# Softmax attention: splits and normalisations on GpSimd, product copies on ScalarE, projections cut into single contractions

## The reference, cut to what matters

```
xn  = layer_norm(x) * w + b
q,k,v = xn @ Wq + bq, xn @ Wk + bk, (xn @ Wv + bv) * mask
y   = softmax(q k^T + (1 - mask) * -big) v          per head
h   = silu(layer_norm(y) * scale(emb) + shift(emb))
out = x + h @ W_out + b_out
```

## Time and profile before

| what | us |
|---|---|
| median of 3 runs | 3429.45 (3423.07 to 3432.16) |
| span of the profiled execution | 3412.4 |
| busy in the span: PE, DVE, ACT, POOL | 2677.2, 2564.3, 2151.3, 1715.5 |
| softmax attention, first x load issued to last result | 1470.9 to 2221.0 |

### The profile page before, as it was taken

How to read it: one execution, slowest core, us unless ns; L and a number is a source line. 1 busy time by engine, 2 the same in 40 slices (tenths; PEclk the granted TensorE clock), 3 DMA queues, 4 the chain that set the end, 5 groups by cost and what they waited for, 6 DMA issues and landing times. The chain is left out here.

```text
span 3412.4 us, 37646 instructions
## 1 busy us (share of the span) xinstructions
PE 2677.2 (78%) x11156; PEld 1441.3 (42%) x11156; DVE 2564.3 (75%) x3375; ACT 2151.3 (63%) x3536; POOL 1715.5 (50%) x1221
## 2 busy tenths in 40 slices
PE   5787588888888888838888888848877788787875
PEld 4555244444444444422333333224444444444443
DVE  2444288888888898947777777538988888888895
ACT  0333478878878778613555555547876776767772
POOL 0000077867768778930000000027887877877785
PEclk9999699999999999967998989969999899989998
DMA  2000101011111111135444444010111111111111
GB/s 89 25 25 31 66 32 51 32 52 49 42 51 40 44 39 52 39 69 82 76 76 76 75 76 70 20 66 32 48 41 58 53 47 53 40 58 51 41 61 45
DMA packets 104194, 176.59 MB, mean 52 GB/s; under 512 B 10741, under 2 KB 91421, under 8 KB 95166
## 3 DMA queue, kind: packets, MB, share of 16 engines
q1 hardware_dynamic: 99775, 161.69, 17.7%
q0 software_dynamic: 4224, 12.59, 1.2%
HBM read 139.70 MB, written 34.14 MB: 51 GB/s over the span
## 5 line engine op out<-in xcount | busy, mean ns | idle before, releaser
L1037 POOL TENSOR_TENSOR l_h<-l_h,l_c_all 128x512 f32<-128x512 f32 x1024 | 1481.3, 1457 | 459.0 <-DVE l_h L966 430.8
L966 DVE TENSOR_TENSOR_SCAN l_h<-l_dA,l_ps_dbu 128x512 f32<-128x512 f32 x1024 | 1218.3, 1207 | 254.1 <-PE l_ps_dbu L1196 157.2
L838 ACT ACTIVATE l_dub<-l_duT,l_b_tok 128x512 f32<-128x512 f32 x1024 | 726.0, 713 | 336.7 <-PE l_ps_dbu L1196 330.6
L1196 PE MATMUL l_ps_dbu<-ident,l_dub 128*128 128x128 f32 x4096 | 644.7, 291 | 257.6 <-DVE l_h L966 175.6
L1196 PEld LDWEIGHTS l_ps_dbu<-ident,l_dub 128*128 128x128 f32 x4096 | 500.7, 148 | 683.6 <-DVE l_h L966 331.9
L852 ACT ACTIVATE l_dA<-l_dt,l_a_neg 128x512 f32<-128x512 f32 x1024 | 726.4, 713 | 0.2
L1628 ACT ACTIVATE l_probs<-l_ring 128x512 f32<-128x512 f32 x512 | 284.2, 598 | 301.4 <-PE l_ring L1752 298.7
L1183 PE MATMUL l_ps_y<-l_h,ident 128*128 128x512 f32 x768 | 430.2, 644 | 51.9 <-DVE l_h L931 51.4
L1461 DVE TENSOR_REDUCE l_q_max<-l_ring 128x1 f32<-128x512 f32 x512 | 327.5, 681 | 144.1 <-PE l_ring L1745 139.4
L996 POOL DMA_INDIRECT l_x_in<-x_dram,l_idx_x x32 | 37.3, 1166 | 735.9 <-DMA l_idx<-in_idx 729.6
L931 DVE TENSOR_TENSOR l_h<-l_h 128x512 f32<-128x512 f32 x384 | 350.5, 916 | 11.8 <-POOL l_h L1037 11.3
(11 more groups left out here) (237 smaller groups left out, 3000.9 us busy)
## 6 DMA issues: line engine op xcount, KB each, us to landing
...
```

The lines of the kernel that those rows point to most:

```text
L838: return act.activation(dub[:, n % 2, t, :], duT[:, p, t, :], ACT.Copy, scale=b_tok[:, p, t, n:n + 1])
L966: dve.tensor_tensor_scan(h[:, h_slot(s), :], dA[:, s % DA_RING, :], ps_dbu[:, dbu_slot(s), :], 0.0, ALU.mult, ALU.add).then_inc(scan_ok, 1)
L1037: pool.tensor_tensor(h[:, h_slot(s), :], h[:, h_slot(s), :], c_all[:, (n // C_GROUP) % 2, n % C_GROUP, :], ALU.mult).then_inc(hc_ok, 1)
L1196: last = pe.transpose(ps_dbu[:, dbu_slot(s), t * P:(t + 1) * P], dub[:, n % 2, t, j * P:(j + 1) * P], ident[:])
```

## The change

All of it lies in `softmax_attention`.

- GpSimd gets a queue of work: the second and third part of each split (`rest_parts`), the same for the maxima (`max_rest`), and both normalisations (`ln_apply`, `ln2_apply`). VectorE keeps the first subtraction of each (`split`, `max_parts`). `rest` has two buffers in place of one.
- `products_out` moves from VectorE to ScalarE.
- `project` is cut into its two contractions k = 0, 1 and `tokens` (for `v_rows` and `project_out`) into its four token blocks; each piece stands behind a step of its own.
- All four lists get new step numbers, which now count single steps s. The SP queue keeps its order. `rows` and `row_rest` become views of `probs`.

```diff
-rest = sb("rest", [P, T])
+rest = sb("rest", [P, DH, T])
...
+def ln_apply(b):
+    pool.wait_ge(rstd_ok, b + 1)
+    pool.sem_inc(passed_p, 1)
+    for t in range(TB):
+        last = pool.tensor_scalar(x_in[:, t, :], x_in[:, t, :], moments[:, t, 0:1], rstd[:, t:t + 1], ALU.subtract, ALU.mult)
+    last.then_inc(xn_ok, 1)
...
+def rest_parts(b, i, g):
+    n = b * 2 * DH + i * DH + g + 1
+    pool.wait_ge(rest_ok, n)
+    pool.sem_inc(passed_p, 1)
+    pool.tensor_copy(parts[:, i, 1, g, :], rest[:, g, :]).then_inc(p2_ok, 1)
+    pool.wait_ge(p2_ok, n)
+    pool.sem_inc(passed_p, 1)
+    pool.tensor_tensor(parts[:, i, 2, g, :], rest[:, g, :], parts[:, i, 1, g, :], ALU.subtract).then_inc(p3_ok, 1)
...
+def max_rest(b, g):
+    n = b * GROUPS + g + 1
+    pool.wait_ge(mr_ok, n)
+    pool.sem_inc(passed_p, 1)
+    pool.tensor_copy(m_parts[:, g, 1, :], m_rest[:]).then_inc(m2p_ok, 1)
+    pool.wait_ge(m2p_ok, n)
+    pool.sem_inc(passed_p, 1)
+    pool.tensor_tensor(m_parts[:, g, 2, :], m_rest[:], m_parts[:, g, 1, :], ALU.subtract).then_inc(m3_ok, 1)
...
+def run(b, p, has_post, has_next, has_after):
+    max_rest(b, 1)
+    if has_after:
+        ln_apply(b + 2)
+    max_rest(b, 2)
+    if has_post:
+        ln2_apply(b - 1)
+    if has_after:
+        rest_parts(b + 2, 0, 0)
+    max_rest(b, 3)
+    if has_after:
+        rest_parts(b + 2, 0, 1)
+    if has_next:
+        max_rest(b + 1, 0)
+    if has_after:
+        rest_parts(b + 2, 1, 0)
+        rest_parts(b + 2, 1, 1)
...
-def ln_stats(b):
-    dve.wait_ge(x_ld, b * 16 + 16)
-    for t in range(TB):
+def ln_stats(b, t2):
+    if t2 == 0:
+        dve.wait_ge(x_ld, b * 16 + 16)
+    for t in (2 * t2, 2 * t2 + 1):
         last = dve.bn_stats(stats[:, t, :], x_in[:, t, :])
-    last.then_inc(st_ok, 1)
+    if t2:
...
-    if not (first(b) and i + g == 0):
-        dve.wait_ge(p3_ok, n - 1)
-    dve.scalar_tensor_tensor(rest[:], halves[g][:], bias, parts[:, i, 0, g, :], ALU.add, ALU.subtract).then_inc(rest_ok, 1)
-    dve.wait_ge(rest_ok, n)
-    dve.tensor_copy(parts[:, i, 1, g, :], rest[:]).then_inc(p2_ok, 1)
-    dve.wait_ge(p2_ok, n)
-    dve.tensor_tensor(parts[:, i, 2, g, :], rest[:], parts[:, i, 1, g, :], ALU.subtract).then_inc(p3_ok, 1)
+    if not (first(b) and i == 0):
+        dve.wait_ge(p3_ok, n - DH)
+    dve.scalar_tensor_tensor(rest[:, g, :], halves[g][:], bias, parts[:, i, 0, g, :], ALU.add, ALU.subtract).then_inc(rest_ok, 1)
...
-def products_out(b, g):
-    n = b * GROUPS + g
-    dve.wait_ge(pv_ok, n + 1)
-    if not (first(b) and g == 0):
-        dve.wait_ge(y_tr, n)
-    dve.tensor_copy(yT[:], ps_y[:]).then_inc(yt_ok, 1)
...
-        if i in (14, 22, 30): products_out(b, i // GU - 1)
-        if i in (16, 24, 31): quotient(b, p, (i + 1) // GU - 2)
-        if i == 2: max_parts(b, 1)
-        if has_after:
-            if i == 4: ln_stats(b + 2)
-            if i == 12: ln_apply(b + 2)
-        if has_post:
-            if i == 6: products_out(b - 1, GROUPS - 1)
-            if i == 8: quotient(b - 1, 1 - p, GROUPS - 1)
-            if i == 9: ln2_stats(b - 1, 1 - p)
-            if i == 11: ln2_apply(b - 1, 1 - p)
-        if i == 10: max_parts(b, 2)
-        if has_post and i in (17, 19): result(b - 1, (i - 17) // 2)
-        if i == 18: max_parts(b, 3)
-        if has_after:
-            if i == 24: split(b + 2, 0, 0)
-            if i == 26: split(b + 2, 0, 1)
-            if i == 27: split(b + 2, 1, 0)
-            if i == 31: split(b + 2, 1, 1)
-        if i == 27 and has_next: max_parts(b + 1, 0)
+            s = 2 * i + half
+            if has_after:
+                if s in (1, 2): ln_stats(b + 2, s - 1)
+                if s == 3: ln_moments(b + 2)
+            if s == 4: max_parts(b, 1)
+            if has_post:
+                if s == 15: quotient(b - 1, 1 - p, GROUPS - 1)
+                if s in (16, 17): ln2_stats(b - 1, s - 16)
+                if s == 18: ln2_moments(b - 1)
+            if s == 19: max_parts(b, 2)
+            if has_after and s == 21: split(b + 2, 0, 0)
+            if s in (31, 47, 63): quotient(b, p, s // (2 * GU) - 1)
+            if has_post and s in (34, 36): result(b - 1, (s - 34) // 2)
+            if s == 39: max_parts(b, 3)
+            if has_next and s == 51: max_parts(b + 1, 0)
+            if has_after:
+                if s == 49: split(b + 2, 0, 1)
+                if s == 53: split(b + 2, 1, 0)
+                if s == 62: split(b + 2, 1, 1)
...
+def products_out(b, g):
+    n = b * GROUPS + g
+    act.wait_ge(pv_ok, n + 1)
+    if not (first(b) and g == 0):
+        act.wait_ge(y_tr, n)
+    act.activation(yT[:], ps_y[:], ACT.Copy).then_inc(yt_ok, 1)
...
-        if has_next and i in (7, 9): v_part(b + 1, 1 - p, (i - 7) // 2)
-        if has_post:
-            if i == 10: ln_rstd(b - 1, moments2, mom2_ok, rstd2, ln_b, rstd2_ok)
-            if i == 14:
+            s = 2 * i + half
+            if has_after and s == 5: ln_rstd(b + 2, moments, mom_ok, rstd, ln_a, rstd_ok)
+            if has_post and s == 11: products_out(b - 1, GROUPS - 1)
+            if has_next and s in (12, 15): v_part(b + 1, 1 - p, (s - 12) // 3)
+            if has_after:
+                if s in (16, 17): xnT_half(b + 2, s - 16)
+                if s == 20: first_part(b + 2, 0, 0)
+            if has_post and s == 21: ln_rstd(b - 1, moments2, mom2_ok, rstd2, ln_b, rstd2_ok)
+            if s in (27, 43, 59): products_out(b, s // (2 * GU) - 1)
+            if has_post and s == 28:
                 for h in range(DH):
                     silu_half(b - 1, h)
-        if has_after:
-            if i == 5: ln_rstd(b + 2, moments, mom_ok, rstd, ln_a, rstd_ok)
-            if i in (19, 20): xnT_half(b + 2, i - 19)
-            if i == 23: first_part(b + 2, 0, 0)
-            if i == 25: first_part(b + 2, 0, 1)
-            if i == 26: first_part(b + 2, 1, 0)
-            if i == 31: first_part(b + 2, 1, 1)
+            if has_after:
+                if s == 47: first_part(b + 2, 0, 1)
+                if s == 51: first_part(b + 2, 1, 0)
+                if s == 61: first_part(b + 2, 1, 1)
...
-def project(b, i, g):
-    if first(b) and i + g == 0:
+def project(b, i, g, k):
+    if first(b) and i + g + k == 0:
         pe.wait_ge(w_ld, 48)
-    pe.wait_ge(xnT_ok, b * DH + DH)
-    take(halves[g], rest_ok, b * 2 * DH + i * DH + g + 1)
+    pe.wait_ge(xnT_ok, b * DH + k + 1)
+    if k == 0:
+        take(halves[g], rest_ok, b * 2 * DH + i * DH + g + 1)
     weight = wq if i == 0 else wk
+    last = pe.matmul(halves[g][:], weight[:, k, g * P:(g + 1) * P], xnT[:, k, :], start=(k == 0), stop=(k == DH - 1),
+                     skip_group_check=True)
+    if k == DH - 1:
+        last.then_inc(qk_mm, 1)
...
-        if has_post and 2 <= i < 2 + TB: times_v(b - 1, 1 - p, GROUPS - 1, i - 2)
-        if i >= GU and 2 <= i % GU < 2 + TB: times_v(b, p, i // GU - 1, i % GU - 2)
-        if i == 1: max_rows(b, 1)
-        if has_post and i == 7: turn(b - 1, GROUPS - 1)
-        if has_next and i in (6, 8): v_rows(b + 1, (i - 6) // 2)
-        if i == 9: max_rows(b, 2)
-        if has_post and i in (12, 13): yn_half(b - 1, 1 - p, i - 12)
-        if i in (15, 23, 31): turn(b, i // GU - 1)
-        if has_post and i in (16, 17): project_out(b - 1, i - 16)
-        if i == 17: max_rows(b, 3)
-        if has_after:
-            if i in (18, 19): xn_half(b + 2, i - 18)
-            if i == 22: project(b + 2, 0, 0)
-            if i == 24: project(b + 2, 0, 1)
-            if i == 25: project(b + 2, 1, 0)
-            if i == 30: project(b + 2, 1, 1)
-        if has_next and i == 26: max_rows(b + 1, 0)
+            s = 2 * i + half
+            if s == 1: max_rows(b, 1)
+            if has_next and s in (0, 2, 12, 14): v_rows(b + 1, (0, 2, 12, 14).index(s))
+            if has_post and s in (4, 6, 8, 10): times_v(b - 1, 1 - p, GROUPS - 1, (s - 4) // 2)
+            if has_post and s == 13: turn(b - 1, GROUPS - 1)
+            if has_after:
+                if s in (15, 16): xn_half(b + 2, s - 15)
+                if s in (18, 19): project(b + 2, 0, 0, s - 18)
+            if s == 17: max_rows(b, 2)
+            if s >= 2 * GU and s % (2 * GU) in (4, 6, 8, 10): times_v(b, p, s // (2 * GU) - 1, (s % (2 * GU) - 4) // 2)
+            if has_post and s in (25, 27): yn_half(b - 1, 1 - p, (s - 25) // 2)
+            if s in (29, 45, 61): turn(b, s // (2 * GU) - 1)
+            if has_post and 32 <= s < 32 + TB: project_out(b - 1, s - 32)
+            if s == 37: max_rows(b, 3)
+            if has_next and s == 49: max_rows(b + 1, 0)
+            if has_after:
+                if s in (44, 46): project(b + 2, 0, 1, (s - 44) // 2)
+                if s in (48, 50): project(b + 2, 1, 0, (s - 48) // 2)
+                if s in (59, 60): project(b + 2, 1, 1, s - 59)
```

121 lines of the change are left out of this document (69 added, 52 removed).

## The result

The changed kernel took 3454.31 us (4 runs, 3447.41 to 3461.93), the kernel before 3427.01 beside it: a ratio of 1.0085, 95% interval 1.0061 to 1.011. That is **slower by 0.85%**, 21 to 38 us. The forecast was 3427.6, no change, with 3450 as its upper end.

The account below looks back on a forecast made before the run. TensorE was taken to lead, VectorE close behind, with a DMA floor before step 32. 1.8 - 7.1 + 5 x (-8.3 + 10.0) - 2.6 - 3.0 + 0.5 = -1.9 took 3429.45 to 3427.6 us; range 3402 to 3450.

Parts of the forecast that it names:

- C: Piece of a body from the first DMA of `stack` to step 32: held by transfers, so no change, 28.5 to 29.5 us.
- the DMA floor: Transfers from `stack` to the split maxima landing at step 32: a bound on C that no faster engine lowers.
- the wait for x: VectorE at the early statistics in bodies 1 to 5: idle 7.6 us until the load of x lands.
- Bodies 6 and 7 and the tail: Bodies without splits or x lose only copy and `ln2_apply` on VectorE: -3, between 0 and -6; tail +0.5.
- Start: Before body 0: normalisation on GpSimd after its fills and slower splits, less a projection and a shorter `max_parts`: +1.8 us.
- Body 0: First body, no wait for x: A -8.3, and +1.2 in B for statistics preceding `max_parts`, together -7.1 us.
- A: Piece from step 32 to the last split: transposes, a projection and pauses go, falling 8.3 to about 38 us.
- B: Piece from the last split to the first DMA of `stack`: +10.0, to 17.0 us against a mean of 7.05.
- smaller waits: Waits between pairs in A that shorter blocks avoid: 0.9 us a body, between 0 and 2.5.
- the handover of 2.1 us: Splits ending on GpSimd: its copy 0.65, subtraction 1.29 and two handovers 0.15 delay the load of x by 2.1 us.
- no relief of A: Slower rival: VectorE, still with splits at steps 49, 53, 62, holds the ring; A falls only 5; 3447 us, chance 0.10.
- The clock: Slower rival: half clock after pauses lasts 8 to 12 us a body, if A exceeds 40; 3442 us, chance 0.15.

Follow-up runs that it names:

- e8: Changed kernel with everything behind the normalisation of y three steps later, that normalisation still on GpSimd: 3429.8 us, 1.0021 of the kernel before.
- e1: Changed kernel with both normalisations (of x and of y) back on VectorE: 3419.8 us, 0.9992 of the kernel before.
- e2: Changed kernel with x loaded a body ahead, normalisations left on GpSimd: 3402.3 us, 0.9933 of the kernel before.
- e3: Changed kernel with both normalisations back on VectorE and x loaded a body ahead: 3375.7 us, 0.9851 of the kernel before.
- e5: Changed kernel with only the normalisation of y back on VectorE, that of x still on GpSimd: 3425.7 us, 1.0014 of the kernel before.
- e4: Kernel before with only the statistics of x moved from behind step 4 to behind step 0: 3459.1 us, 1.0105 of the kernel before.
- e9: e3 with its single contractions and token blocks joined again into larger blocks: 3393.9 us, 0.9918 of the kernel before.

## Why the prediction was wrong

- **C** ("the DMA floor stays: 0", the floor ending last by an estimated 2): **this step failed.** C was 32.4, 3 us more, five times 3 = 15 of the 16 by which bodies 1 to 5 were missed. The floor is there (29.4 in e8), but the step counted only what moves on TensorE and forgot the normalisation of y, which feeds its transposes at steps 25 and 27. It was moved to GpSimd and given no duration of its own anywhere in the body. The slack of 2 wasn't there either. With y back in time (e1) the Silu block, and not the floor, still ends C at 30.0; without the wait for x C falls to 30.2 (e2), without both to 28.2 (e3). So the slow clock behind the wait for x, which the floor was to swallow, reached into C.
- **Bodies 6 and 7 and the tail** (-3 and +0.5): +13.9, of which e1 takes back 14.3 and e5, with y alone, 13.7. The same omission: the work was booked as one that VectorE loses, not as one that TensorE waits for. The tail alone has a wait of 8.4 us for 4.8 before.
- **Start** (+1.8): +3.7 up to step 0 of body 0 (104.0 for 100.3). "For doing it then" had been given 1.8 us, where GpSimd needs 4.84, twice; over nine profiles the normalisation of x on GpSimd costs some 6 us there (e5).
- **Body 0** (-7.1): -3.1, or -4.1 by the prediction's own count. This isn't the normalisation: e1 leaves the body at 78.0 (76.4 changed, 79.5 before). The stack starts 2.8 us later behind step 0 where 1.2 was charged (11.9 for 9.1), the maxima then land 29.9 behind it for 29.5, and A falls by 7.3 by that count in place of 8.3.
- **B** (+10.0; 17.0 including the 2.1, so 14.9 from `parts_out`): 14.8 to 15.5. The wait for x, forecast at 7.6, was 7.62. Right. e4 shows the same from the other side.
- **A** (down 8.3 to about 38, counted to VectorE's last part): 41.4 to `parts_out` in body 4, 39.3 by that count, and 38.4 in e3. Right in kind, 1.6 short in size: in the mean of bodies 1 to 5 it fell by 6.7 (46.0 to 39.3). B had been compared with 7.05, the mean of two bodies; over all five it was 7.8 before, so it grew by 1.3 less than forecast. The two misses nearly cancel, and that is luck. The 0.9 us for smaller waits in A was well sized: e9 puts it at 0.8. What e9 shows beyond it, 2.0 a body in B and C, the prediction gave no price.
- The sum also leaves out, once, the handover of 2.1 us at the border into body 6, where no wait for x stands. With it the sum is +0.2 and the forecast the same case.
- The price itself: a TENSOR_SCALAR of this size, with two operands per partition, stands in no GpSimd row of the trace before. It should have been bounded as the copy was, from 0.25 (half of the 512-column bound, by the fill) up to 0.63, half of the subtraction's 1.25. Even that would have been too low: measured 1.22 us for 256 columns (median of 32), as much as the subtraction over 512. Four of 0.63 are 2.5 us, and the room in the body was about 2.8 (4.84 less the wait of 2.05), so naming the step would have shown the risk, but not the wait. On VectorE the same takes, in e1 (ns, least, median, most):

```profile
L1532 DVE TENSOR_SCALAR l_y<-l_y,l_moments,l_rstd x32: 399/406/1250, 1691.2 to 2223.2; 128x256 f32<-128x256 f32 x32
```

The Trainium skill (GPSIMD Engine Reference, § 4.1 Engine selection) says that elementwise work with one input is roughly at line rate on GpSimd and only that with two inputs about twice slower. The measurement differs: with one tensor and two operands per partition GpSimd takes three times VectorE's 0.406. The plain copy of 512 columns does fit it, 0.61 beside the 0.69 of VectorE's copy of products.

Of the rivals that end slower, "no relief of A" didn't come about: A had most of its relief. "The clock" did in part. Behind the stall at the Silu block TensorE stood at 0.50 for 7.7 us and more in body 4 (1971.30 to 1979.00), where it was 5.2 before, near the 8 at the low end of its range. But its own conditions weren't met (A at 39.3 where it needed 40, the wait for x at 7.6 where it needed 8.5), and in e1, with the normalisations on VectorE, the slow stretch is 6 us and a body is within 0.3 us of the sum's figure. Neither rival names the wait for y. With the normalisations on VectorE, which is the kernel that the sum in effect described, the stage came out at +3.5 us and the time at 0.9992: the forecast of no change was right for e1, helped by misses of opposite sign in A and B, and the missing term was 33 us of the stage.
